# Row maxima of the scores split into 16-bit parts and turned once a batch, between the key projections, with the score row turned later in the batch

## The reference

```python
q = rms_norm(linear(x, q_w, q_b), norm_q_w).reshape(B, L, NH, HD)              # 16 heads of 32
k = rms_norm(linear(ctx_txt, k_w, k_b), norm_k_w).reshape(B, -1, NH, HD)       # 118 text rows
v = linear(ctx_txt, v_w, v_b).reshape(B, -1, NH, HD)
k_img = rms_norm(linear(ctx_img, k_img_w, k_img_b), norm_k_img_w).reshape(B, -1, NH, HD)   # 257 image rows
v_img = linear(ctx_img, v_img_w, v_img_b).reshape(B, -1, NH, HD)
img_x = attention(q, k_img, v_img)
txt_x = attention(q, k, v)
x = x + linear((txt_x + img_x).reshape(B, L, DIM), o_w, o_b)
```

## Time and profile before

| | |
|---|---|
| three runs | 1525.77, 1529.79, 1529.23 us, median 1529.23 |
| the profiled execution | 1524.64 us, of which span 1522.9 us |
| granted TensorE clock | 0.999 of full |
| PE busy | 1497.2 us, 98% |
| DVE, ACT, POOL busy | 78%, 47%, 45% |
| chain that ended last | PE 89%, DVE 5%, ACT 3% |

### The profile page before, as it was taken

How to read it: one execution, slowest core, us unless ns; L and a number is a source line. 1 busy time by engine, 2 the same in 40 slices (tenths; PEclk the granted TensorE clock), 3 DMA queues, 4 the chain that set the end, 5 groups by cost and what they waited for, 6 DMA issues and landing times.

```text
span 1522.9 us, 41381 instructions
## 1 busy us (share of the span) xinstructions
PE 1497.2 (98%) x16220; PEld 1186.7 (78%) x16220; DVE 1182.6 (78%) x1884; ACT 715.8 (47%) x1458; POOL 688.5 (45%) x727
## 2 busy tenths in 40 slices
PE   8999999999999999999999999999999999999997
PEld 6777777777777777777777777777777787778997
DVE  6765788888888888888888888888887686554986
ACT  5874444444444444444444444444445124655431
POOL 3543344454444454444444444544445692114752
PEclk9999999999999999999999999999999999999999
DMA  8961121211111221112221112121125524010000
GB/s 262 346 207 60 39 63 52 77 56 50 56 54 59 67 66 50 56 50 62 62 70 50 56 50 62 58 75 50 56 87 154 196 111 167 28 56 29 1 1 25
DMA packets 70199, 121.04 MB, mean 79 GB/s; under 512 B 21840, under 2 KB 36528, under 8 KB 68608
## 3 DMA queue, kind: packets, MB, share of 16 engines
q1 hardware_dynamic: 69312, 117.54, 23.9%
q0 software_dynamic: 832, 2.75, 0.7%
HBM read 89.93 MB, written 30.34 MB: 79 GB/s over the span
## 4 chain that ended last, share of the span: by engine, by line
PE 89%; DVE 5%; ACT 3%; issue 1%; DMA 1%; POOL 1%; ACTq 0%; DVEq 0%; POOLq 0%
PE ps L1535 21%; PE ps L1536 19%; PE ps L1537 18%; PE ps L1691 10%; PE ps L1654 6%; PE ps L1625 3%; PE ps L1596 3%; PE ps L1660 2%; PE ps L1900 2%; PE ps L1917 2%; PE ps L1909 1%; PE ps L1664 1%; DMA q_dram<-q_turned 1%; DVE rec L1163 1%; PE ps L1636 0%
## 5 line engine op out<-in xcount | busy, mean ns | idle before, releaser
L547 POOL TENSOR_TENSOR ctx_lo<-ctx_raw,ctx_hi 128x472 fp32r<-128x472 f32 (+1 forms) x62 | 112.8, 1819 | 192.8 <-ACT ctx_hi L780 192.8
L1163 DVE RECIPROCAL rec<-ps 128x224 f32<-128x224 f32 x128 | 198.3, 1549 | 1.1 <-PE ps L1691 0.9
L581 POOL TENSOR_TENSOR prob_img<-prob 128x448 f32<-128x448 f32 x93 | 107.9, 1160 | 149.3 <-ACT prob L845 149.3
L1152 DVE TENSOR_REDUCE top<-ps 112x4 f32<-112x1028 f32 x128 | 156.2, 1220 | 0.0
L1151 DVE TENSOR_REDUCE top<-ps 112x4 f32<-112x472 f32 x128 | 83.1, 649 | 72.9 <-PE ps L1625 72.9
L1654 PE MATMUL ps<-q_all,k_all 32*128 32x112 f32 (+1 forms) x3072 | 125.2, 274 | 0.0
L1535 PE MATMUL ps<-w_v_img_hi,ctx_hi 128*128 128x512 f32 x256 | 107.4, 419 | 0.0
L1535 PE MATMUL ps<-w_k_img_hi,ctx_hi 128*128 128x512 f32 x256 | 107.1, 418 | 0.0
L843 ACT ACTIVATE prob<-ps 119x448 f32<-119x448 f32 x96 | 52.4, 546 | 114.8 <-PE ps L1654 114.8
L1654 PEld LDWEIGHTS ps<-q_all,k_all 32*128 32x128 f32 (+1 forms) x3072 | 105.4, 184 | 0.0
L1536 PE MATMUL ps<-w_k_img_lo,ctx_hi 128*128 128x512 f32 x256 | 101.1, 395 | 0.0
(11 more groups left out here) (358 smaller groups left out, 4410.7 us busy)
## 6 DMA issues: line engine op xcount, KB each, us to landing
ctx_raw<-in_ctx_dram SPq DMA_DIRECT2D x32, 748.0 KB, 4.2
xh_dram<-xh SPq DMA_DIRECT2D x32, 448.0 KB
xc<-in_xT_dram SPq DMA_DIRECT2D x28, 256.0 KB, 4.5
q_dram<-q_turned SPq DMA_DIRECT2D x28, 256.0 KB, 4.6
q_all<-q_dram SPq DMA_DIRECT2D x32, 224.0 KB, 3.1
out_dram<-out_sb SPq DMA_DIRECT2D x32, 224.0 KB, 2.3
xh<-in_x_dram SPq DMA_DIRECT2D x31, 224.0 KB, 2.9
proj<-in_x_dram SPq DMA_DIRECT2D x21, 256.0 KB, 5.1
```

The costliest lines, as they stand in the source:

```text
L547: nc.gpsimd.tensor_tensor(ctx_lo[:, :, cols], ctx_raw[:, :, cols], ctx_hi[:, :, cols].bitcast(F32), ALU.subtract).then_inc(ctx_lo_done, 1)
L581: nc.gpsimd.tensor_tensor(prob_img[:, g % 2], image[:, 0, :], image[:, 1, :], ALU.add).then_inc(img_summed, 1)
L1152: nc.vector.tensor_reduce(rows[:, :, 2 * g + 1], ps[0:L, 2:6, TAIL:CTX], AX.X, ALU.max).then_inc(s_done, 1)
L1163: nc.vector.reciprocal(rec[:], bank[:, 2:4]).then_inc(norm_step, 1)
```

## The change

- The maxima of all four groups go to one tile `top`, 32 columns for each head position: columns 0 to 7 hold the maxima (`top` is 112 x 128). When group 3 is done, DVE rounds the 32 used columns to 16 bits (`top_hi`) and writes the rest, maximum minus rounded part, to columns 8 to 15 (`split_top`, two instructions).
- PE turns the tile once (`turn_top(i)`), ACT copies it once to a 16-bit `topT`. The selection matrices are 16-bit, with -1 in two rows, so that one matmul adds both parts. In each `scores_T` the two selections now stand ahead of all products.
- On PE the one turn stands behind `keys(n, 0)`; behind it come the first three matmuls (chunk 0) of `keys(n, 1)`, then `scores_T(i, 0)`, then the other nine.
- The score row is turned after the output product of p, ahead of the turns of the new keys, into bank 2, one of the score banks; `ranks` on DVE moves from ahead of `scale_k(n, 1)` to behind `add_tail(i, 2)`. PE waits for the ranks at the end of the batch.
- In the last batch the score row is turned right behind the maxima, and on POOL `residual(p)` moves ahead of the splitting of value weights.

```diff
-        pick_c = p1("pick_c", [P, NG, CHUNK_C], F32R)
-        pick_img = p1("pick_img", [P, NG, P], F32R)
+        pick_c = p1("pick_c", [P, NG, CHUNK_C], BF16)
+        pick_img = p1("pick_img", [P, NG, P], BF16)
...
-        top = [p1(f"top{e}", [L, P]) for e in range(2)]
-        topT = [p1(f"topT{e}", [P, L], F32R) for e in range(2)]
+        top = p1("top", [L, P])
+        topT = p1("topT", [P, L], BF16)
+        top_hi = p1("top_hi", [L, GH * 2 * NG], BF16)
...
@@ gpsimd, last
                 output(q)
+                residual(p)
                 pool.wait_ge(oT_lo_done, i)
+                pool.wait_ge(top_split, i + 1)
                 value_weights_lo(0, 0)
+                normalise_h(p)
                 value_weights_lo(0, 1).then_inc(w_lo_done, 1)
-                residual(p)
-                normalise_h(p)
@@ scalar
-            def turn_top(i, e):
-                act.wait_ge(top_full, 2 * i + e + 1)
-                nc.scalar.activation(topT[e][:], ps[:, 6, e * L:(e + 1) * L], ACT.Copy).then_inc(topT_ready, 1)
+            def turn_top(i):
+                act.wait_ge(top_full, i + 1)
+                nc.scalar.activation(topT[:], ps[:, 6, 0:L], ACT.Copy).then_inc(topT_ready, 1)
@@ vector
+            def split_top(i):
+                rows = top[:].rearrange("l (j r) -> l j r", j=GH)
+                high, low = rows[:, :, 0:2 * NG], rows[:, :, 2 * NG:4 * NG]
+                dve.wait_ge(s_done, 4 * i + 4)
+                nc.vector.tensor_copy(top_hi[:].rearrange("l (j r) -> l j r", j=GH), high).then_inc(top_rounded, 1)
+                dve.wait_ge(top_rounded, i + 1)
+                nc.vector.scalar_tensor_tensor(low, high, 1.0, top_hi[:].rearrange("l (j r) -> l j r", j=GH), ALU.mult, ALU.subtract).then_inc(top_split, 1)
@@ vector, body
                 group_max(i, 3)
+                split_top(i)
...
                 add_tail(i, 0)
-                if q is not None:
-                    ranks(q)
                 scale_k(n, 1)
...
                 add_tail(i, 2)
+                if q is not None:
+                    ranks(q, ps[0:L, 2, 0:L])
                 tail_keys(n)
@@ tensor, scores_T
-                    nc.tensor.matmul(ps[0:CHUNK_C, 2 + j, 0:L], pick_c[head, g, :], topT[g // 2][head, :], start=True, stop=False)
-                products(0, True)
+                    nc.tensor.matmul(ps[0:CHUNK_C, 2 + j, 0:L], pick_c[head, g, :], topT[head, :], start=True, stop=False)
                 for j in range(GH):
                     head = slice(HD * j, HD * (j + 1))
                     nc.tensor.matmul(ps[:, 2 + j, L:3 * L].rearrange("p (c q) -> p c q", c=2), pick_img[head, g, :],
-                                     topT[g // 2][head, :].unsqueeze(1).to_broadcast([HD, 2, L]), start=True, stop=False)
+                                     topT[head, :].unsqueeze(1).to_broadcast([HD, 2, L]), start=False, stop=False)
+                products(0, False)
                 products(1, False)
                 products(2, True).then_inc(st_full, 1)
@@ tensor, body
                 values(i, 1)
-                turn_top(i, 0)
                 scores(i, 3)
                 keys(n, 0)
-                turn_top(i, 1)
+                turn_top(i)
+                keys(n, 1, range(0, 1))
                 scores_T(i, 0)
-                keys(n, 1)
-                if q is not None:
-                    pe.wait_ge(pv_done, 4 * i)
-                    turn_score(q)
+                keys(n, 1, range(1, KC))
...
                 weighted_values(i, 0, n)
-                if q is not None:
-                    pe.wait_ge(rank_done, q + 1)
                 weighted_values(i, 1, n)
...
                 pe.wait_ge(exp_done, 8 * i + 8)
+                if q is not None:
+                    turn_score(q, ps[0:L, 2, 0:L])
                 for k in range(1, 4):
                     turn(n, k)
...
                 values(n, 0, range(2 if p is None else 0, KC))
+                if q is not None:
+                    pe.wait_ge(rank_done, q + 1)
@@ tensor, last
-                turn_top(i, 1)
+                turn_top(i)
+                pe.wait_ge(pv_done, 4 * i)
+                turn_score(q, late_score_row)
                 scores_T(i, 0)
-                pe.wait_ge(pv_done, 4 * i)
-                turn_score(q)
```

More of the change, by code:

```diff
@@ L1374, in _ @@
             hT_rest(3)
-            ranks(B - 2)
+            ranks(B - 2, late_score_row)
             def add_value_bias(m):
@@ L1579, in turn_q, with keys @@
                 last.then_inc(q_turn_full, 1)
[L1581 removed]
+            def keys(n, k, chunks=range(KC)):
                 cols, w, rows = ((slice(0, TXT), "k", TXT), (slice(TXT, TXT + P), "k_img", P), (slice(TXT + P, CTXC), "k_img", P))[k]
[L1584 to L1585 removed]
                 full, done, bank, slot = key_slot(n, k + 1)
[L1587 to L1589 removed]
+                if 0 in chunks:
+                    if k < 2:
+                        pe.wait_ge(ctx_lo_done, 2 * n + k + 1)
+                    if not isinstance(n, int) or n or k == 2:
+                        pe.wait_ge(done, slot)
+                last = project(bank[0:rows], ctx_hi, ctx_lo, cols, w, chunks)
+                if KC - 1 in chunks:
+                    last.then_inc(full, 1)
             def turn(n, k):
```

60 lines of the change are left out of this document (26 added, 34 removed).

## The result

The changed kernel takes 1643.7 us (median of 4 runs, 1640.97 to 1644.09), the kernel before 1527.9 us (median of 4 runs): a ratio of 1.0753, 95% interval 1.0739 to 1.0767. It is slower by 116 us. The direction was forecast; the size, 1547 us with a range to 1555, was missed by almost 100 us.

What follows compares the result with a forecast made beforehand. PE, busy 98% of the span, was taken as the bound. A loop batch gains 0.65 us, 29 of them 18.9, with the other batches 20.3: 1544.9 or 1549.5 us by base, forecast 1547, range 1538 to 1555.

Steps and rivals of the forecast that it cites:

- wait on `ctx_lo`: First image keys, ahead of `scores_T(i, 0)`: PE waits for POOL's part 1, making `scores_T(i, 1)` 0.54 us later a batch.
- The split: DVE's rounding after the last maxima: takes at most 0.73 us, ends at 562.98 or earlier, before PE's turn at 563.11.
- signs of being wrong: Changed profile: no idle time before image keys, `scores_T` under 1.0 us, or DVE-ended idle time ahead of `scores(i, 1)` or turn.
- `normalise(p, 3)` and `add_bias(n, 1)`: On DVE, up to 0.7 us later; costed at nothing because their ACT users stand behind the later exponentials of group 0.
- The ranks at the end of DVE's batch: `ranks` moved to the end of DVE's batch: its 0.73 us uses up 0.77 us of idle time, costing PE nothing.
- Rival 4: Late maxima on DVE or later `ctx_lo` add a second wait; with 0.3 us a batch, 1556 us; chance 0.15.
- main case: Wait of about half a microsecond a batch, selections as fast as now: 1543 to 1551 us; chance 0.60.
- The selections at 0: Selection matmuls in `scores_T`: 16-bit types save nothing, within bounds of 0 and 0.22 us a group.
- rival 1: In `scores_T`, the 128-column selection load gets fast: 0.06 to 0.07 us saved a group, 1539 us; chance 0.16.
- second rival: By its number: both selection loads in `scores_T` get fast and outweigh the wait, 1519 us; chance 0.04.
- One turn fewer: On PE ahead of `scores(i, 3)`: removing the turn of tile 0 saves 0.11 us a batch.
- The copy of `topT`: ACT's copy after the turn, 0.26 us long: done at 563.7, ahead of its use at 564.75, "a second to spare".

Runs made afterwards that it cites:

- experiment 6: Kernel before with only the first chunk of the image keys issued ahead of `scores_T(i, 0)`, the other three behind it; 1604.6 us.
- experiment 7: Kernel before with the image keys divided around `scores_T(i, 0)` and POOL's `residual` moved behind `inverse_rms(n, 3)`; 1549.6 us, ratio 1.0151.
- experiment 3: Changed kernel with the image keys whole behind `scores_T(i, 0)`, as before the change; 1571.9 us.
- experiment 8: Changed kernel with only POOL's `residual` moved behind `inverse_rms(n, 3)`; 1565.2 us.
- experiment 5: Changed kernel with the image keys whole behind `scores_T(i, 0)` and without the split of the maxima; 1527.5 us.
- experiment 12: Kernel before with one maxima tile, no split, one turn ahead of the last `keys(n, 0)` chunk, 16-bit selections in new order; keys whole, ranks unmoved; 1511.4 us.
- experiment 10: Kernel before with only the selection matrices and turned maxima in 16 bits, old order and two turns kept; 1518.4 us, ratio 0.9949.

## Why the prediction was right in sign and wrong in size

The step that failed is the price of the first image keys ahead of `scores_T(i, 0)`. The sum had the wait on `ctx_lo` for it, 0.54 us a batch, and nothing for what the moved keys do to POOL and, through POOL, to DVE. By itself that edit costs 78 us (experiment 6), of which 22 are the forecast wait with its passages and 55 the collision (experiment 7). The split, forecast as hidden, costs 17 to 44 us more, by what stands beside it. The sign did not need luck, for the forecast wait is real. The prediction's signs of being wrong named idle time "ahead of `scores(i, 1)` or of the turn, ended by DVE"; that held for two of the three waits that came; the longest it did not name.

- *The wait on `ctx_lo`* (+0.54 us a batch, "part 1 ends 10.58 us behind the second score group"). Right as a mechanism and close in size: 10.56 us in the changed kernel (611.86 - 601.30), 0.53 us of wait without the split, 0.44 in the kernel before with the keys divided. With the collision taken out the divided keys cost 22 us, where the prediction's sum for the whole change was 20. In the changed kernel the wait cannot be seen, because the turn ahead of it waits longer.
- *The split* (at most 0.73 us, hidden). This failed too. The price came from two small instructions that met no POOL instruction; here the cast starts inside `ctx_lo`, whose 2.42 us stood in the earlier trace rows, right beside the maxima of the earlier trace rows. Start to end the split is 1.85 us (610.26 to 612.11). It costs 44 us beside whole keys (1571.9 against 1527.5), 17 beside divided ones.
- *`normalise(p, 3)` and `add_bias(n, 1)`, "so I cost them at nothing", and nothing at all on `scale_k`.* The step that failed most: 72 us of the 116 come back with whole keys, 79 with `residual` later. I had counted what the shorter way from `scores_T(i, 0)` to `scores_T(i, 1)` does to PE and to ACT's copies, but not to POOL. `sum_image(i, 0)`, and `residual` two instructions behind it, hang on `scores_T(i, 0)`, which comes later by the wait and the key chunk; `sum_image(i, 1)` hangs on `scores_T(i, 1)`, which comes later by the wait alone. Measured from a batch's first score group, `sum_image(i, 0)` starts at 15.73 us before and at 17.13 in experiment 6, the exponentials of group 1 at 18.35 and 19.04: 1.40 and 0.69 us later. The 0.7 us between are more than POOL's gap of 0.54 us, and DVE's `scale_k` had no place to get in. From there the delay runs over `rstd` to `add_tail(i, 1)`. The earlier trace rows held a hint: the 0.94 us of `scale_k(n, 1)` there end 0.55 us behind `residual`, and alone it takes 0.75 (experiment 7), so it was already held up for 0.2 us in the kernel before. Experiments 3 and 6 put this on the divided keys, 7 and 8 on the neighbourhood of the two POOL instructions.
- *The ranks at the end of DVE's batch* ("uses that idle time up and does not pass on"; rival 4 with 0.3 us). Rival 4 was right, together with the main case and not in its place: `scores` waits 0.3 us a batch without the collision (experiment 8), and 0.6 us in 16 of the 28 batches of the loop in the changed kernel. With whole keys the wait does not occur in the loop (experiments 3 and 5), so the ranks there cost something only in a DVE batch that is late already.
- *The selections at 0.* Wrong; rival 1's price of 0.06 to 0.07 us a group was right for the type (0.065), but not its condition. With the new order in both, 16 bits take the step from `pick_c` (119 columns) to the next start from 0.15 to 0.10 us, and that from `pick_img` (128) from 0.16 to 0.10. The new order adds 0.047. In all 0.112 us a group, 14 us, which hid part of the loss. (The rule on 128 columns, which the prediction calls its second rival, is its first.)
The Trainium skill ("TensorE: Matmul & The Clock Gate", section "Weight-path perf modes — Fast Weight Load (FWL) and DoubleRow") has the fast load for 128 weights of a type other than FP32. The runs neither show that load nor rule it out: the 119-column selection quickened nearly alike, and the recorded loads fell alike too, from 173 to 125 ns and from 187 to 130 (128 columns) from the kernel before to the changed one; how much of the gain is the load's and how much the moving side's, which is 16-bit too, they don't separate.
- *One turn fewer* (-0.11 us). Right: experiment 12 has 32.78 - 4 x 0.112 - 0.11 = 32.22 by the terms and 32.20 to 32.23 in the trace.
- *The copy of `topT`, "a second to spare"* (a microsecond). True only with a key chunk between turn and selection; without it PE waits 0.45 us a batch for it, 14 us in the run of experiment 5. Experiment 12 has no such wait and is 16 us faster, but it has the ranks at their old place too.

The periods of the loop close the account, each from one trace: 32.78 before; 33.88 with `residual` later, which is the turn later by its wait (+1.05: 1.29 us from the last key matmul to the turn where it was 0.24), the wait of `scores` (+0.3) and the passages of the divided keys (+0.26), less the selections (-0.45) and one turn (-0.11), 33.83 in all; 36.2 with the collision at a full clock; 36.5 with the clock's falls. Why the clock falls in one batch of three, and not in each, stays open.

What held DVE up is a rule of the Trainium skill as well ("SBUF — State Buffer", section "Who interferes with whom"): DVE and GpSimd share one pair of ports under an exclusive lock held for a whole instruction. DVE's casts in their two-port modes contend for it, and DVE instructions with two SBUF inputs do against a GpSimd instruction that reads SBUF; those with at most one SBUF input, outside these modes, don't. The trace agrees at each place: the cast waits (1.63 us, 0.17 alone), `scale_k` with `proj` and `w_txt` waits (2.78 us, 0.75 alone), and `add_tail` too (1.56, 0.68), while the maxima, read from PSUM, take 1.22 us with `ctx_lo` beside them as without, and the ranks of the kernel before, with their scores in PSUM, 0.33 us inside `residual` (568.52). The skill speaks of one blocked instruction. What decided here is that the wait goes on over a second POOL instruction if that starts without a gap.

## What to carry to other kernels

On DVE and POOL price an added instruction with two SBUF inputs, or a cast, by the POOL instruction that it will start inside, and not by its own length; a length far above that of its shape, ending with or half a microsecond behind a POOL instruction, is a wait. When work leaves the stretch between two events on PE, look at what the other engines do there: a gap of a few tenths between two POOL instructions can be what keeps DVE on time, and moving one of the two took back 55 of 78 us and 79 of 116. Here the divided keys were still not worth having: without them and the split the kernel is faster than before. Try the parts of a bundled change alone: three of this one's pay (one turn, 16 bits, the order with them), and the two that cost most (the split, the divided keys) are not needed for them.

## What the runs showed of the hardware

- A DVE instruction held up by POOL stays held up over back-to-back POOL instructions (2.78 us over 1.50 and 1.15), and gets in through a gap of 0.34 us. Where DVE starts first it is POOL's instruction that gets longer (1.16 to 1.52 us, experiment 7).
- Two 16-bit selections next to each other are 0.047 us a group faster than with 32-bit products between them; with all in 32 bits the order makes no difference. In experiment 10 the products between them start 0.10 us behind `pick_c` (0.15 before) but take 0.25 us to the start of `pick_img` (401.58 to 401.83; 0.18 before): the stretch up to the switch back to 16 bits is 0.07 us longer, all that the first set had gained.
- After idle times of about 1.8 us on PE the granted clock fell to 0.5 for 3.41 us in 13 of some 30 batches; with matmuls in those idle times, in one. But it fell four times too in a loop without an idle time over 0.91 us (experiment 3). The net price of twelve falls was 8 us, not the 20 us that 12 x 3.41 / 2 gives.
